# Front stage of an attention and expert kernel: query and key rows stored by three transfers each, weights on ScalarE's queue, VectorE's first work reordered

## The chip, the cores and the metric

The kernel runs on one core of one Trainium2 chip. A core has TensorE (PE in the profile), VectorE (DVE), ScalarE (ACT), GpSimd (POOL) and SyncE (SP); each has a queue of its own instructions, taken in the order in which they are written, and they meet through semaphores. SP and ACT can also issue DMAs, which move data between the chip's memory (HBM) and the core's on-chip memory (SBUF). The metric is the device time of one execution in microseconds (us); the time given for a kernel is the median of several executions that are not profiled.

## The reference

Two sequences of 1024 tokens with 128 channels go through one transformer layer. Attention has 16 heads of 8 channels, is causal, and each score gets a rank-one bias; the second half is a mixture of seven experts, of which each token takes two, with a shared expert.

```python
def _L0_attn_ref(x, w_qkv, w_out, head_scales, head_dirs):
    q, k, v = split_heads(x @ w_qkv)
    scores = jnp.einsum('bhqd,bhkd->bhqk', q, k) * SCALE
    q_proj = jnp.einsum('bhtd,hd->bht', q[..., :8], head_dirs)
    k_proj = jnp.einsum('bhtd,hd->bht', k[..., :8], head_dirs)
    scores = where(causal, scores, -inf) + head_scales * q_proj[..., :, None] * k_proj[..., None, :]
    return merge_heads(softmax(scores) @ v) @ w_out
...
x = x + _layernorm(_L0_attn_ref(_layernorm(x), ...))
x = x + _layernorm(_L0_ffn_ref(_layernorm(x), ...))   # router, top 2 of 7 experts, shared expert
```

## The kernel before, in words

There are two blocks, one after the other. The first holds the front stage and the attention, the second the projection of the second sequence, the router and the experts. The change is in the front stage.

**The front stage.** SP loads x in two transfers, one for each sequence b, and then six weights (L246, L250). VectorE's first instruction (L664, `dirs_scaled`) waits for all six. Then it computes the variances of sequence 0 (`variances(0)`, L673 to L678), folds the bias into the query weights with two small matmuls of TensorE (L391, L394; `fold`, `wq_fold`), normalises the tokens of sequence 0 (`normalise_tokens`, L691, tile `xn_stage`) and does `variances(1)` and `normalise_tokens(1)`. TensorE turns the tokens (L406), ScalarE takes them (L588, `xn_t`), and TensorE makes queries, keys and values (L415, L417, L422) for each sequence and each half of 512 tokens.

**The split in three.** Each float32 query or key is written as a sum of three bfloat16 numbers. ScalarE takes the high part (L595, L597), VectorE the middle and the low one with three instructions (L718, L721, L723), one round for the queries and one for the keys of each of four (b, half): eight rounds in all. `parts_ready` rises once for each (b, half). A product of two such numbers is kept to six of the nine pairs of parts (`COMBOS`), so each head has rows of 8 channels times 6 pairs, 48 in all, for queries and for keys, and one bfloat16 matmul over 48 rows gives a score.

**Through HBM.** The parts lie with channels on partitions; a matmul needs the 48 rows of one head on neighbouring partitions. So SP stores the parts to two arrays in HBM, `q_rows` and `k_rows` (`store_parts`, L256: six transfers for queries and six for keys of one (b, half), of 128 KB each, one for each pair), and loads them again as stacks (`load_stacks(n, c)`, L265: four transfers for a group n of four heads and a half c of the tokens). A load waits until all stores of its (b, half) have landed (`parts_stored`).

**The attention.** For each group n, TensorE first forms the scores with queries on partitions (`maxima`, L444 to L450), and VectorE takes the maximum of each row (L749). The maxima are turned, GpSimd splits them in three parts (`split_rows`, L355 to L360), and SP writes them as three more rows of the query stacks (`send_rows(n, c)`, L275: six transfers of 2 KB). Then TensorE forms the scores again with keys on partitions, less the maxima (`score`, L461), ScalarE takes exponentials (L611), and TensorE multiplies with the values (L480). Twelve units x make up a group: units 0 to 3 need the queries of half 0, units 4 to 11 those of half 1. The maxima of group 0 are formed ahead of everything else; those of group n + 1 are formed between the scores of group n. Before its first maxima TensorE waits until all splits are done (`parts_ready`, L536).

**The order of SP's queue** is written out by hand:

```python
store_parts(0, 0)
sp.wait_ge(ones_ready, STACKS)
load_stacks(0, 0)
store_parts(0, 1)
load_stacks(0, 1)
load_stacks(1, 0)
load_stacks(1, 1)
send_rows(0, 0)
for half in range(2):
    store_parts(1, half)
send_rows(0, 1)
```

Meanwhile GpSimd clears tiles (`v_pad`, `k_st`) and makes masks, until 18.8 us.

Of the kernel before, what the change touches and what calls it, by code (L numbers as in the profile page):

```python
# [16 lines left out]
BF16 = mybir.dt.bfloat16  # L17
U32 = mybir.dt.uint32
ALU = mybir.AluOpType
# [3 lines left out]
B, T, C, H = 2, 1024, 128, 16  # L23
HD = C // H
SCALE = 1.0 / float(np.sqrt(HD))
P = 128
KT = T // P
NT = B * KT
HG = 4
# [4 lines left out]
COMBOS = ((0, 0), (0, 1), (0, 2), (1, 0), (1, 1), (2, 0))  # L34
KR = HD * len(COMBOS)
MR = KR + 3
HALF = P // 2
BANK = 512
# [77 lines left out]
def program(nc, x, wqkv, wq_t, dirs, scales, w_out, router_t, w_gate, w_up, w_down, out):  # L116
    ctx = ExitStack()
    with ctx:
# [10 lines left out]
        q_rows = nc.dram_tensor("q_rows", [B * H, KR, T], BF16, kind="Internal").ap()  # L129
        k_rows = nc.dram_tensor("k_rows", [B * H, KR, T], BF16, kind="Internal").ap()  # L130
# [4 lines left out]
        w_out_sb = sb("w_out_sb", [C, C])  # L135
        router_sb = sb("router_sb", [C, E])
# [13 lines left out]
        wqkv_sb = sb_front("wqkv_sb", [C, 3 * C])  # L150
        wq_t_sb = sb_front("wq_t_sb", [C, C])
        wq_fold = sb_front("wq_fold", [C, C])
        dirs_sb = sb_front("dirs_sb", [1, C])
        scales_sb = sb_front("scales_sb", [1, H])
        dirs_scaled = sb_front("dirs_scaled", [1, C])
# [10 lines left out]
        rest = x2[:, :, :].rearrange("p t c -> p (t c)").rearrange("p (h i t) -> p h i t", h=2, i=2)  # L166
# [17 lines left out]
        def bank(i, n=1):  # L184
            return banks[:, i * BANK:(i + n) * BANK]
# [11 lines left out]
        vector_steps = sem("vector_steps")  # L197
# [46 lines left out]
        def _(sp):  # L244
# [3 lines left out]
            for dst, src in ((dirs_sb[:, :], dirs), (scales_sb[:, :], scales), (wq_t_sb[:, :], wq_t),  # L248
                             (wqkv_sb[:, :], wqkv), (w_out_sb[:, :], w_out), (router_sb[:, :], router_t)):
                sp.dma_start(dst, src).then_inc(weights_loaded, 16)  # L250

            def store_parts(b, half):
                sp.wait_ge(parts_ready, b * 2 + half + 1)
                for qk, dst in ((0, q_rows), (1, k_rows)):
                    for row, combo in enumerate(COMBOS):
                        sp.dma_start(  # L256
                            dst[b * H:(b + 1) * H, row * HD:(row + 1) * HD, half * BANK:(half + 1) * BANK],
                            parts[b][:, half, qk, combo[qk], :]).then_inc(parts_stored[b * 2 + half], 16)

            def load_stacks(n, c):  # L260
                r, b = n % STACKS, n // NG
                sp.wait_ge(parts_stored[b * 2 + c], 16 * 2 * len(COMBOS))
                for dst, src in ((q_st[r], q_rows), (k_st[r], k_rows)):
                    for a in range(2):
                        sp.dma_start(  # L265
                            dst[a * HALF:a * HALF + KR, c, :, :],
                            src[n * HG:(n + 1) * HG, :, c * BANK:(c + 1) * BANK].rearrange(
                                "(p a) r t -> a r p t", a=2)[a]).then_inc(stacks_loaded[r][c], 16)
# [119 lines left out]
        def _(pe):  # L388
# [10 lines left out]
            for b in range(B):  # L399
# [9 lines left out]
                for half in range(2):  # L409
# [3 lines left out]
                    if done >= 2:  # L413
                        pe.wait_ge(parts_ready, done - 1)
# [121 lines left out]
            pe.wait_ge(parts_ready, 4)  # L536
# [41 lines left out]
        def _(act):  # L578
            def standard_deviations(b):
                act.wait_ge(var_ready, b + 1)  # L580
                part = slice(b * KT, (b + 1) * KT)
                nc.scalar.activation(std[:, part], var_eps[:, part], ACT.Sqrt).then_inc(std_ready, 1)

            standard_deviations(0)
# [76 lines left out]
        def _(dve):  # L661
            step = Count()
            dve.wait_ge(weights_loaded, 16 * 6)
            nc.vector.tensor_tensor(dirs_scaled[:, :].rearrange("o (h d) -> o h d", d=HD),  # L664
                                    dirs_sb[:, :].rearrange("o (h d) -> o h d", d=HD),
                                    scales_sb[:, :].unsqueeze(2).broadcast_to([1, H, HD]),
                                    ALU.mult).then_inc(dirs_scaled_ready, 1)
# [28 lines left out]
            variances(0)  # L696

# [11 lines left out]
            variances(1)  # L709
            normalise_tokens(1)  # L710
            for b in range(B):
                for half in range(2):
                    for qk in range(2):
                        src = bank(4 * half + 1 + qk)
                        high, mid, low = (parts[b][:, half, qk, i, :] for i in range(3))
                        left = rest[:, half, qk, :]
                        dve.wait_ge(high_ready, b * 4 + half * 2 + qk + 1)
                        nc.vector.tensor_tensor(left, src, high, ALU.subtract  # L718
                                                ).then_inc(vector_steps, step.one())
                        dve.wait_ge(vector_steps, step.now())  # L720
                        nc.vector.tensor_copy(mid, left).then_inc(vector_steps, step.one())  # L721
                        dve.wait_ge(vector_steps, step.now())
                        last = nc.vector.tensor_tensor(low, left, mid, ALU.subtract)  # L723
                    last.then_inc(parts_ready, 1)
# [833 lines left out]
```

## Time and profile before

| | |
|---|---|
| time, median of 3 executions | 524.5 us (523.02 to 527.57) |
| span of the profiled execution | 542.4 us |
| TensorE busy | 440.5 us (81% of the span) |
| VectorE busy | 329.6 us (61%) |
| ScalarE busy | 244.3 us (45%) |
| GpSimd busy | 142.2 us (26%) |
| DMAs of SP's queue for `q_rows` and `k_rows` | 48 of 128 KB |
| first score of group 0 (L461) | 67.0 us from the span's start |

The profiled execution was 17.9 us longer than the median of the executions without a profile. Busy times are those of one execution. All stretches below are counted from the span's start; the front stage and the first group's maxima fill roughly its first 67 us, the other groups run until about 315 us, the experts until the end.

### The profile page before, as it was taken

The numbers are of one execution on the slowest core, as the hardware profiler recorded it, in microseconds if no ns is written. First come the engines' busy times: TensorE is split into PE (matmuls) and PEld (weight loads), VectorE is DVE, ScalarE is ACT, GpSimd is POOL, SyncE is SP. The second block draws the span as 40 slices with busy tenths as digits, with TensorE's granted clock in tenths as the row PEclk, the third lists the DMA queues.
The fourth block names the chain that finished last, engine by engine and source line by source line (L and its number), as shares of the span: only waits on it lengthen the run. The fifth ranks groups of instructions, "written<-read, shape, count | busy, mean of one in ns | idle before, by whom it ended". The sixth has DMA issues, their size and how long they took to land. (4 is left out here: it accounts for less than half of the span.)

```text
span 542.4 us, 10816 instructions
## 1 busy us (share of the span) xinstructions
PE 440.5 (81%) x3980; PEld 267.0 (49%) x3980; DVE 329.6 (61%) x885; ACT 244.3 (45%) x432; POOL 142.2 (26%) x211
## 2 busy tenths in 40 slices
PE   1845978989898998999898968888699989898800
PEld 0522432434434352434434345645499889888800
DVE  3975956868787876878782764599223322223356
ACT  1520145666665765677675827552122222213330
POOL 9300000010111101011111002424626665573423
PEclk9975576999989997999988988999979999999965
DMA  3065254100202020000000008100447768766352
GB/s 102 21 179 150 78 157 119 58 5 3 60 2 61 2 60 2 2 3 3 3 2 2 1 2 232 39 2 1 160 137 228 205 194 215 215 206 190 98 160 78
DMA packets 44616, 46.60 MB, mean 86 GB/s; under 512 B 6355, under 2 KB 33364, under 8 KB 44564
## 3 DMA queue, kind: packets, MB, share of 16 engines
q1 hardware_dynamic: 42132, 40.92, 25.8%
q0 software_dynamic: 2432, 4.99, 3.6%
q8 instruction: 33, 0.54, 0.4%
q14 instruction: 19, 0.16, 0.1%
HBM read 34.80 MB, written 10.88 MB: 84 GB/s over the span
## 5 line engine op out<-in xcount | busy, mean ns | idle before, releaser
L611 ACT ACTIVATE probs<-banks 128x1024 f32<-128x1024 f32 (+1 forms) x192 | 145.3, 810 | 80.6 <-PE banks L468 52.5
L749 DVE TENSOR_REDUCE mx_part<-banks 128x1 f32<-128x512 f32 (+3 forms) x256 | 133.2, 584 | 42.1 <-PE banks L444 34.2
L444 PE MATMUL banks<-k_st,q_st 48*128 48x512 bf16 (+3 forms) x384 | 123.9, 370 | 14.5 <-DMA k_st<-k_rows 12.3
L461 PE MATMUL banks<-q_st,k_st 51*128 51x512 bf16 (+3 forms) x384 | 103.7, 349 | 17.7 <-DMA q_st<-mx_rows 11.3
L480 PE MATMUL banks<-probs,v_pad 128*32 128x512 f32 (+3 forms) x768 | 86.8, 526 | 0.0
L461 PEld LDWEIGHTS banks<-q_st,k_st 51*128 51x128 bf16 x384 | 32.1, 96 | 75.7 <-ACT probs L611 49.9
L749 DVE TENSOR_REDUCE mx<-banks 128x1 f32<-128x512 f32 (+3 forms) x128 | 54.7, 485 | 20.1 <-PE banks L450 20.0
L1488 DVE TENSOR_TENSOR hidden<-banks,gate 128x512 f32<-128x512 f32 x38 | 26.3, 692 | 61.6 <-ACT gate L1256 28.8
L355 POOL TENSOR_TENSOR mx_rest<-mx_neg,mx_rows 16x128 f32<-16x128 f32 x16 | 6.7, 417 | 199.2 <-ACT mx_neg L621 199.2
L444 PEld LDWEIGHTS banks<-k_st,q_st 48*128 48x128 bf16 x384 | 34.7, 95 | 43.6 <-DVE mx_part L749 24.8
L448 PE MATMUL banks<-mask_qk,ident_half 64*128 64x128 bf16 x256 | 56.2, 232 | 0.0
L1024 POOL DMA_INDIRECT results<-result,target x38 | 37.4, 984 | 49.9 <-DVE result L1496 44.3
L466 PE MATMUL banks<-mask_kq,ident_half 64*128 64x128 bf16 x256 | 49.8, 221 | 0.0
L450 PE MATMUL banks<-mask_qk,ident_half 64*128 64x64 bf16 x256 | 49.1, 198 | 0.0
L1155 PE MATMUL banks<-rows_t,w_g 128*128 128x128 f32 x304 | 42.1, 282 | 4.4 <-issue 3.9
L468 PE MATMUL banks<-mask_kq,ident_half 64*128 64x64 bf16 x256 | 44.1, 190 | 0.0
L1164 PE MATMUL banks<-w_d,hidden 128*128 x304 | 41.0, 278 | 3.2 <-DVE hidden L1488 2.8
L1155 PE MATMUL banks<-rows_t,w_u 128*128 128x128 f32 x304 | 41.4, 279 | 0.5 <-issue 0.5
L1016 POOL DMA_INDIRECT rows<-tokens,source x38 | 36.8, 969 | 19.0 <-issue 11.0
L1155 PEld LDWEIGHTS banks<-rows_t,w_g 128*128 128x128 f32 x304 | 37.7, 195 | 6.8 <-issue 5.9
L1249 ACT ACTIVATE rows_t<-banks 128x128 f32<-128x128 f32 x38 | 10.6, 279 | 65.3 <-PE banks L1143 45.3
L1164 PEld LDWEIGHTS banks<-w_d,hidden 128*128 128x128 f32 x304 | 37.5, 194 | 4.0 <-issue 4.0
(198 smaller groups left out, 616.1 us busy)
## 6 DMA issues: line engine op xcount, KB each, us to landing
w_g<-in_w_gate SPq DMA_DIRECT2D x38, 256.0 KB
w_u<-in_w_up SPq DMA_DIRECT2D x38, 256.0 KB
q_rows<-parts SPq DMA_DIRECT2D x24, 128.0 KB, 2.4
k_rows<-parts SPq DMA_DIRECT2D x24, 128.0 KB, 2.4
q_st<-q_rows SPq DMA_DIRECT2D x32, 96.0 KB, 2.3
k_st<-k_rows SPq DMA_DIRECT2D x32, 96.0 KB, 2.3
w_d<-in_w_down SPq DMA_DIRECT2D x8, 256.0 KB, 4.9
back<-results SPq DMA_DIRECT2D x8, 256.0 KB, 4.8
```

Source lines behind the costliest of these rows:

```text
L444: last = nc.tensor.matmul(dst[:, 0:width], q_st[r][rows, c, p, (i % CH) * P:(i % CH + 1) * P], k_st[r][rows, kc, p, 0:width], start=True, ...
L448: nc.tensor.matmul(dst[:, diagonal:width], ident_half[half, 0, :], mask_qk[half, 0, :], start=False, stop=False)
L450: last = nc.tensor.matmul(dst[:, diagonal + HALF:width], ident_half[half, 1, :], mask_qk[half, 1, HALF:], start=False, stop=True)
L461: last = nc.tensor.matmul(dst[a][:, 0:width], k_st[r][rows, j // CH, p, (j % CH) * P:(j % CH + 1) * P], q_st[r][rows, c, p, first:BANK], s ...
L466: nc.tensor.matmul(dst[a][:, 0:P], ident_half[half, 1, :], mask_kq[half, 1, :], start=False, stop=False)
L468: last = nc.tensor.matmul(dst[a][:, 0:HALF], ident_half[half, 0, :], mask_kq[half, 0, 0:HALF], start=False, stop=True)
L480: last = nc.tensor.matmul(o_bank[h * HQ:(h + 1) * HQ, first:BANK], v_pad[:, n, j, h, :], probs[unit % PROBS][:, h, first:BANK], start=(x i ...
L611: nc.scalar.activation(probs[unit % PROBS][:, 2 * p:2 * p + 2, first:BANK], slot_pair[k % 2].rearrange("p (a t) -> p a t", a=2)[:, :, 0:BA ...
L749: nc.vector.tensor_reduce(dst, max_bank[m % RING][:, 0:width], AX.X, ALU.max, negate=True).then_inc(max_taken, 1)
L1024: nc.gpsimd.indirect_dma_start(results, bass.IndirectOffsetOnAxis(ap=target[:, k:k + 1], axis=0), result[i][:, :], None).then_inc(result_s ...
L1155: last = nc.tensor.matmul(dst[k % 2][:, t * P:(t + 1) * P], w[i][:, t * P:(t + 1) * P], rows_t[k % 2][:, :], start=True, stop=True)
L1164: last = nc.tensor.matmul(down_bank[k % 2][:, 0:P], hidden[k % 2][:, t, :], w_d[:, bass.ds(e, 1), t, :].rearrange("p e c -> p (e c)"), sta ...
```

## The change

- `store_parts` issues three transfers for the queries and three for the keys of one (b, half), not six and six (`RUNS`: 3, 2 and 1 pairs). The pairs of one run share the query's part, so that part is read 3, 2 or 1 times by a source that repeats; the key's parts of a run lie side by side in SBUF. The bytes that are written stay the same. The arrays in HBM are laid out by channel and pair now, and the loads of the stacks read the same number of rows of 1024 bytes.
- `parts_ready` rises after the queries and again after the keys, and the stores of the queries no longer wait for the keys' split.
- The six weights are issued by ScalarE's queue, not by SP's behind x.
- VectorE does `variances(0)` first and then waits for the weights; the split of the first (b, half) goes ahead of `normalise_tokens(1)`.

```diff
+RUNS = ((0, 3), (3, 2), (5, 1))
...
-        q_rows = nc.dram_tensor("q_rows", [B * H, KR, T], BF16, kind="Internal").ap()
-        k_rows = nc.dram_tensor("k_rows", [B * H, KR, T], BF16, kind="Internal").ap()
+        q_rows = nc.dram_tensor("q_rows", [B * C, len(COMBOS), T], BF16, kind="Internal").ap()
+        k_rows = nc.dram_tensor("k_rows", [B * C, len(COMBOS), T], BF16, kind="Internal").ap()
...
-            for dst, src in ((dirs_sb[:, :], dirs), (scales_sb[:, :], scales), (wq_t_sb[:, :], wq_t),
-                             (wqkv_sb[:, :], wqkv), (w_out_sb[:, :], w_out), (router_sb[:, :], router_t)):
-                sp.dma_start(dst, src).then_inc(weights_loaded, 16)
-
             def store_parts(b, half):
-                sp.wait_ge(parts_ready, b * 2 + half + 1)
                 for qk, dst in ((0, q_rows), (1, k_rows)):
-                    for row, combo in enumerate(COMBOS):
-                        sp.dma_start(
-                            dst[b * H:(b + 1) * H, row * HD:(row + 1) * HD, half * BANK:(half + 1) * BANK],
-                            parts[b][:, half, qk, combo[qk], :]).then_inc(parts_stored[b * 2 + half], 16)
+                    sp.wait_ge(parts_ready, b * 4 + half * 2 + qk + 1)
+                    rows = dst[b * C:(b + 1) * C, :, half * BANK:(half + 1) * BANK]
+                    for at, count in RUNS:
+                        if qk == 0:
+                            src = parts[b][:, half, 0, COMBOS[at][0], :].unsqueeze(1).broadcast_to([P, count, BANK])
+                        else:
+                            src = parts[b][:, half, 1, 0:count, :]
+                        sp.dma_start(rows[:, at:at + count, :], src).then_inc(parts_stored[b * 2 + half], 16)
...
-                sp.wait_ge(parts_stored[b * 2 + c], 16 * 2 * len(COMBOS))
+                sp.wait_ge(parts_stored[b * 2 + c], 16 * 2 * len(RUNS))
...
-                            src[n * HG:(n + 1) * HG, :, c * BANK:(c + 1) * BANK].rearrange(
-                                "(p a) r t -> a r p t", a=2)[a]).then_inc(stacks_loaded[r][c], 16)
+                            src[n * HG * HD:(n + 1) * HG * HD, :, c * BANK:(c + 1) * BANK].rearrange(
+                                "(p a d) r t -> a (d r) p t", a=2, d=HD)[a]).then_inc(stacks_loaded[r][c], 16)
...
                     if done >= 2:
-                        pe.wait_ge(parts_ready, done - 1)
+                        pe.wait_ge(parts_ready, 2 * (done - 1))
...
-            pe.wait_ge(parts_ready, 4)
+            pe.wait_ge(parts_ready, 8)
...
+            for dst, src in ((dirs_sb[:, :], dirs), (scales_sb[:, :], scales), (wq_t_sb[:, :], wq_t),
+                             (wqkv_sb[:, :], wqkv), (w_out_sb[:, :], w_out), (router_sb[:, :], router_t)):
+                act.dma_start(dst, src).then_inc(weights_loaded, 16)
             standard_deviations(0)
...
             variances(0)
+            scale_directions()
...
             normalise_tokens(0)
             variances(1)
+            split_parts(0, 0)
             normalise_tokens(1)
...
+            split_parts(0, 1)
+            split_parts(1, 0)
+            split_parts(1, 1)
```

`scale_directions` is the old first instruction of VectorE with its wait for the weights; `split_parts(b, half)` is the old pair of rounds for one (b, half), with `parts_ready` raised at the end of each round.

## Rows read from the trace of the kernel before

**Rows 1.** The page: the span; TensorE's granted clock in 40 slices.

```profile
span 542.4 us, 10816 instructions
...
PEclk9975576999989997999988988999979999999965
```

**Rows 2.** Timeline, TensorE: start, us, instruction [idle before <-what ended it].

```profile
29.91 1.05 PE L422 MATMUL banks<-wqkv_sb,xn_t 128*128 128x128 f32 x8
37.72 0.62 PE L444 MATMUL banks<-k_st,q_st 48*128 48x512 bf16 x2 [6.75 <-DMA k_st<-k_rows]
...
50.56 1.03 PE L444 MATMUL banks<-k_st,q_st 48*128 48x512 bf16 x3 [5.54 <-DMA k_st<-k_rows]
...
83.34 0.58 PE L461 MATMUL banks<-q_st,k_st 51*128 51x512 bf16 x1 [5.13 <-DMA q_st<-mx_rows]
```

**Rows 3.** Timeline, SP's queue: start, us until all are issued.

```profile
24.43 3.86 SPq L256 DMA_DIRECT2D q_rows<-parts  x6
28.33 3.86 SPq L256 DMA_DIRECT2D k_rows<-parts  x6
34.03 0.83 SPq L265 DMA_DIRECT2D q_st<-q_rows  x2
...
46.68 0.78 SPq L265 DMA_DIRECT2D q_st<-q_rows  x2
...
57.18 4.20 SPq L275 DMA_DIRECT2D q_st<-mx_rows  x6
61.42 3.80 SPq L256 DMA_DIRECT2D q_rows<-parts  x6
...
78.10 4.06 SPq L275 DMA_DIRECT2D q_st<-mx_rows  x6
```

**Rows 4.** Timeline, VectorE, 7 to 36 us.

```profile
7.82 0.28 DVE L664 TENSOR_TENSOR dirs_scaled<-dirs_sb,scales_sb 1x128 f32<-1x128 f32 x1 [7.82 <-DMA router_sb<-in_router_t]
...
10.37 1.01 DVE L678 TENSOR_SCALAR var_eps<-mean_var 128x8 f32<-128x8 f32 x1
...
13.05 2.68 DVE L691 TENSOR_SCALAR xn_stage<-x_sb,mean_var,rstd 128x128 f32<-128x128 f32 x8
...
18.68 2.14 DVE L691 TENSOR_SCALAR xn_stage<-x_sb,mean_var,rstd 128x128 f32<-128x128 f32 x8
20.74 0.68 DVE L718 TENSOR_TENSOR x<-banks,parts 128x512 f32<-128x512 f32 x1
...
34.44 0.69 DVE L723 TENSOR_TENSOR parts<-x,parts 128x512 bf16<-128x512 f32 x1
```

**Rows 5.** Tile x_sb: its loads' issue (ns) and landing.

```profile
L246 SPq DMA_DIRECT2D x_sb<-in_x x2: 450/511/572, 0.8 to 1.3; - x2
...
DMA to landing us min/median/max: 4.2/4.8/5.5
```

**Rows 6.** Timeline, GpSimd.

```profile
10.40 3.65 POOL L319 MEMSET v_pad<- 128x1024 f32 x4
...
71.94 0.42 POOL L360 TENSOR_TENSOR mx_rows<-mx_rest,mx_rows 16x128 bf16<-16x128 f32 x1
```

**Rows 7.** Timeline, ScalarE, 0 to 36 us.

```profile
18.80 0.60 ACT L595 ACTIVATE parts<-banks 128x512 bf16<-128x512 f32 x1 [0.40 <-PE banks L415]
20.24 0.60 ACT L597 ACTIVATE parts<-banks 128x512 bf16<-128x512 f32 x1 [0.84 <-PE banks L417]
```

**Rows 8.** Windows: engines' busy us (PE first), granted clock, DMA share, GB/s.

```profile
28.00:30.00 2.00, 1.88 (x5) 0.95 (x6) 1.93 (x4) 1.36 (x5) 0.00 (x0) 1.00 0.75 210
...
537.00:538.00 1.00, 0.00 (x0) 0.00 (x0) 1.00 (x4) 0.00 (x0) 0.00 (x0) 0.50 0.94 273
```

**Rows 9.** Timeline, TensorE: first scores of three units (0/7, 1/4, 1/7).

```profile
93.46 0.39 PE L461 MATMUL banks<-q_st,k_st 51*128 51x512 bf16 x1
...
115.78 0.37 PE L461 MATMUL banks<-q_st,k_st 51*128 51x512 bf16 x1 [1.65 <-DMA q_st<-mx_rows]
...
124.11 0.39 PE L461 MATMUL banks<-q_st,k_st 51*128 51x512 bf16 x1
```

More of the change, by code:

```diff
@@ L662, in _, with scale_directions @@
             step = Count()
[L663 to L667, printed above, removed]
+            def scale_directions():
+                dve.wait_ge(weights_loaded, 16 * 6)
+                nc.vector.tensor_tensor(dirs_scaled[:, :].rearrange("o (h d) -> o h d", d=HD),
+                                        dirs_sb[:, :].rearrange("o (h d) -> o h d", d=HD),
+                                        scales_sb[:, :].unsqueeze(2).broadcast_to([1, H, HD]),
+                                        ALU.mult).then_inc(dirs_scaled_ready, 1)
             def variances(b):
@@ L709, in _, with split_parts @@
             variances(1)
-            normalise_tokens(1)
[L711 to L724, printed above, removed]
+            def split_parts(b, half):
+                for qk in range(2):
+                    src = bank(4 * half + 1 + qk)
+                    high, mid, low = (parts[b][:, half, qk, i, :] for i in range(3))
+                    left = rest[:, half, qk, :]
+                    dve.wait_ge(high_ready, b * 4 + half * 2 + qk + 1)
+                    nc.vector.tensor_tensor(left, src, high, ALU.subtract
+                                            ).then_inc(vector_steps, step.one())
+                    dve.wait_ge(vector_steps, step.now())
+                    nc.vector.tensor_copy(mid, left).then_inc(vector_steps, step.one())
+                    dve.wait_ge(vector_steps, step.now())
+                    nc.vector.tensor_tensor(low, left, mid, ALU.subtract).then_inc(parts_ready, 1)
+            split_parts(0, 0)
+            normalise_tokens(1)
+            split_parts(0, 1)
+            split_parts(1, 0)
+            split_parts(1, 1)
             def merge_maxima(n):
```

## The prediction

> **What bounds the kernel now.** The chain of work that ended last reaches back only to the second block, so what the front stage costs is read from TensorE's own waits. Its timeline comes first: three times in the first 84 us it stands still for a DMA, 6.75 us before its first maxima, 5.54 us before the maxima of the second half and 5.13 us before unit 4 of group 0, 17.4 us in all [rows 2]. The first two are ended by the loads of the stacks, the third by the rows of maxima that SP sends.
>
> Then SP's queue, to see why each came late. *First wait:* the twelve stores of (0, 0) are issued from 24.43 to 32.19 us, 0.64 us each; the queue wakes from their landing at 34.03, 1.84 us after the last issue; TensorE starts 3.69 us later [rows 2, 3]. *Second:* the same with (0, 1); the loads go out at 46.68 and TensorE starts 3.88 us later. *Third:* GpSimd has the rows ready at 71.94 + 0.42 = 72.36 us [rows 6], but SP issues them at 78.10, since from 61.42 on it works through the 24 stores of sequence 1 [rows 3].
>
> Last, what paces a store. During the stores the 16 DMA engines are busy 0.75 of the time and move 210 GB/s; near the end of the kernel one store of 512 KB reaches 273 GB/s at 0.94 [rows 8]. So the engines have room, and the issue is what a store waits for. An issue's length doesn't follow its rows: the loads of x, of 1024 rows of 512 bytes (8 tiles by 128 partitions), took 0.45 and 0.57 us [rows 5], a store of 128 rows 0.64.
>
> After the front stage TensorE is the engine that the others wait for, and later SP loads wait for its progress (`slot_filled`). So I carry a shift of group 0 through to the end, one for one.
>
> **The change part by part.**
>
> *Weights on ScalarE's queue, variances first.* VectorE starts at 7.82 us, when the weights are there; the first x has landed at about 0.8 + 4.2 = 5.0 us [rows 4, 5]. The statistics of sequence 0 take from 8.10 to 10.37, 2.3 us, and now lie under the weights' load. ScalarE issues six small loads at up to 0.57 us each [rows 5], 3.4 us, ahead of a square root that it can't start before about 7.5; that hides them. Against it: the same bytes share the same engines, and if x landed as late as the weights nothing would be gained. What is late next is GpSimd. The 8-column `var_eps` took 1.01 us and ended at 11.38, just behind the first of four `v_pad` memsets of 0.91 us that begin at 10.40; the first eight `xn_stage` took 2.68 us, overlapping only the last memset, the second eight 2.14 [rows 4, 6]. Begun two microseconds earlier, the first eight meet three memsets. Of 2.3 us I keep 0.9 (bounds 0.3 and 1.9: all but the memsets' tail lost, or one wait of about 0.4 us).
>
> The Trainium skill's page "SBUF — State Buffer", section "Who interferes with whom", says that a VectorE instruction of such a kind and a GpSimd instruction exclude each other for the whole of the one that was issued first. Read strictly, with each `xn_stage` held by the next memset, only the 0.3 us would remain by my estimate, and the gain below would be 0.6 us less; the rows show the waiting, not how many pass between two memsets.
>
> *The first split ahead of `normalise_tokens(1)`.* ScalarE has the first high query part at 18.80 + 0.60 = 19.40 us and the key's at 20.84 [rows 7]; VectorE took them at 20.74, after the second `xn_stage`. Eight rounds run from 20.74 to 35.13, 1.80 us each [rows 4]. New, in the old clock: queries 19.45 to 21.25, keys to 23.05, then the reciprocal and eight `xn_stage` (2.3 us) to 25.4, then six rounds to 36.2. Less 0.9 that is 35.3, against 35.13 before. This matters, since TensorE's first maxima also wait for all splits (L536), a wait that the loads cover today, until 37.72. It is the next thing to be late: TensorE starts at about 35.4, and only 2.3 of the first 6.75 us are won.
>
> *Half as many stores.* Query stores of (0, 0) can start at 21.25 - 0.9 = 20.3 us. One (b, half) is 1.57 MB, 5.8 us at 273 GB/s [rows 8]; six issues at 0.64 take 3.9 and fit under that. Landing: 20.3 + 5.8 + 1.84 = 27.9. Four loads, twice 0.83 and gaps, go out until 29.7 and have landed by 31.6, hidden under the splits until 35.4. Stores of (0, 1): 29.7 + 5.8 + 1.84 = 37.3, loads landed 3.88 later, 41.2. TensorE's first-half maxima took from 37.72 to 50.56 - 5.54 = 45.02, 7.3 us, so they end at 42.7: the second wait goes, with 1.5 us to spare. Call X the start of the second-half maxima: 50.56 before, 42.7 now. **Gain so far 7.8 us** (2.3 and 5.5).
>
> *The third wait.* All of it is counted from X. The sends of (0, 0) go out at X + 6.6 and the stores of sequence 1 start at X + 10.9 as before [rows 3]; 3.15 MB at 273 GB/s keep the engines until X + 22.4, not the queue until X + 27.5. The rows of (0, 1) are split at X + 21.8 and land with TensorE's start 5.24 us after their first issue, at X + 27.0 to 27.6. TensorE comes to unit 4 at 83.34 - 5.13 = 78.21, X + 27.65. So hardly a wait is left; I leave 1.65 us, which the same place costs in group 1, where SP has nothing else to do [rows 9]. **Gain 3.5 us** (up to 5.1).
>
> *TensorE's clock.* Units 4 to 6 of group 0 took 10.12 us (83.34 to 93.46), those of group 1 8.33 [rows 2, 9]. The granted clock was at its lower level, 1.2 GHz, for most of the former's slice (digit 6) and at the upper for the latter's [rows 1]; it had fallen after the third wait. Without that wait it may stay up, worth 0 to 1.8 us: **0.9**.
>
> *The rest.* The two layouts in HBM give the loads the same rows of 1024 bytes at the same steps, so I price them at nothing; the repeated source costs reads in SBUF of bytes that were read as often before. `parts_ready` counts twice as fast with the same meaning.
>
> Sum: 7.8 + 3.5 + 0.9 = 12.2 us. The profiled execution would span 542.4 - 12.2 = 530.2. It lies 17.9 us above the median of 524.5, and no row tells where; I take the microseconds as they are: 524.5 - 12.2 = **512.3**.
>
> **The rivals.**
>
> *Issue time follows the rows.* 0.64 us for 128 rows and 0.42 for 96 (a load, [rows 3]) are both near 5 ns a row; then three transfers take as long as six, 7.7 us for a (b, half). For it: that ratio. Against: x's 1024 rows in half a microsecond, and the 273 GB/s store. Then X = 20.3 + 7.7 + 1.84 + 1.85 + 7.7 + 1.84 + 3.88 = 45.1, a gain of 5.4, and the third wait stays but for some 0.6 us: 524.5 - 6.0 = 518.5. It decides above 6.5 us for a (b, half), where the second wait returns.
>
> *TensorE slow on sequence 1.* It now waits some 2 us for the second `xn_stage`. If the clock fell there as it does after 29.91 + 1.05 (digit 7, then 5 [rows 1, 2]), three steps of about 1 us for each half double and the splits end at about 38.0: X = 45.4, 2.7 less, 515.0. Against: there it fell after the whole of TensorE's work had ended; here work lies on both sides of the gap.
>
> *The waits are the profile's.* The 17.4 us of waits and the 17.9 us between span and median are strangely alike. If executions without a profile didn't have these waits, nothing would be won: 524.5. Against: they follow from issues of 0.64 us, one after the other, which need no profiler.
>
> *Slower: the query transfers run on few engines.* Their source repeats a row 3, 2 or 1 times. If the count, not the 128 partitions, spread a transfer over the engines, one engine would carry a third of 384 KB, half of 256 and all of 128, 384 KB in all; at 210 / 0.75 / 16 = 17.5 GB/s [rows 8] that is 22.5 us for a (b, half) in place of 5.8. With D for that time X = 29.7 + 2D and unit 4 starts at X + 16.1 + 2D: 135.8 against 83.34, so 52 us more, 577. The two meet at D = 9.4 us, or 167 GB/s: with nine engines or fewer the change loses. Against: the source as written has its 128 partitions outermost, the repeat behind them. The Trainium skill, "DMA: Bandwidth & Descriptors", section "Why a DMA increments its semaphore by 16 and not by 1", has such a rule: the slowest dimension of both sides sets how many of the 16 engines take part. By it 128 partitions give all 16; no row here shows a transfer that repeats its source.
>
> **How the numbers follow.** Forecast 0.60, rows 0.17, slow TensorE 0.12, profile's waits 0.07, few engines 0.04. The forecast's own bounds are 10.7 us (0.3 for the start, no clock) and 15.7 (1.9, 5.1 and 1.8), so 508.8 to 513.8; the shown runs differ by up to 3 us from their median, which widens the low end to 507. To leave out no more than two in ten the range goes up to the first rival: 507 to 519. One per cent, 5.2 us, is about what a measurement of this kernel can tell from no change. Faster by more: the forecast and nearly all of the two next, 0.87. Within: 0.08. Slower: 0.05.
>
> **What would show it.** Right: stores with six issues of about 0.6 us and some 270 GB/s; the first loads issued near 28 us; TensorE's first maxima near 35.4, released by VectorE's last split, not by a load; no wait in front of the second-half maxima; the first sends of (0, 1) within a microsecond of GpSimd's last split; unit 4 after at most 1.7 us. Wrong: issues of 1 us and more (rows), splits with gaps for ScalarE's parts (clock), a DMA share far below 0.9 during the query stores (engines), or units of later groups that take longer than before and give the shift back.

## The result, and the profile of the changed kernel

The changed kernel took 508.58 us (median of 5, 507.37 to 519.39) against 523.02 us in the same session (5, 518.91 to 527.57): ratio 0.9736, 95% interval 0.9679 to 0.9794. A second series gave 506.95 against 525.78 us, 0.9666 (0.9615 to 0.9717). The forecast was 512.3 us, range 507 to 519. Some executions of either kernel are longer at a lower mean clock, the first profiled one of the changed kernel among them (519.39 us; 0.890, c1 0.924); the ratios leave them out, the medians don't (without them the second series has 523.6 us for the kernel before).

Below, c1 is the changed kernel once more, from the second series; its profiled execution took 507.31 us, and all rows of the changed kernel are those of c1. Up to the start of group 1 the two traces of the changed kernel agree within 0.9 us (90.22 and 89.33 there); in later groups they part by more. So stages are compared up to there only, and each trace is one execution: a difference of less than 0.9 us between the points of two traces proves nothing by itself.

The page of c1, its span and the granted clock in 40 slices of 12.6 us:

```profile
span 505.6 us, 10792 instructions
...
PEclk9995589979999899999999996999999999999955
```

TensorE's timeline of c1, with the points that answer to [rows 2, 9]: first maxima, maxima of the second half (X), units 4 and 7 of group 0, group 1.

```profile
35.23 0.40 PE L444 MATMUL banks<-k_st,q_st 48*128 48x512 bf16 x2 [4.22 <-DVE parts L727]
...
42.21 1.05 PE L444 MATMUL banks<-k_st,q_st 48*128 48x512 bf16 x3
...
69.94 0.39 PE L461 MATMUL banks<-q_st,k_st 51*128 51x512 bf16 x1
...
78.17 0.39 PE L461 MATMUL banks<-q_st,k_st 51*128 51x512 bf16 x1
...
89.33 0.39 PE L461 MATMUL banks<-q_st,k_st 51*128 51x512 bf16 x1
```

Of the three waits one is left, and what ends it is no longer a load but VectorE's last split (L727). The other two rows carry no bracket. Group 1 began at 104.62 us before:

```profile
104.62 0.39 PE L461 MATMUL banks<-q_st,k_st 51*128 51x512 bf16 x1
```

So 15.3 us are won by its start. They divide at the same points as in the forecast: 8.35 at X (50.56 to 42.21), 5.05 more at unit 4 (83.34 to 69.94), 1.89 more at unit 7 (93.46 to 78.17), and nothing behind it.

SP's queue of c1, against [rows 3] (start, us until all are issued):

```profile
20.41 1.57 SPq L258 DMA_DIRECT2D q_rows<-parts  x3
22.19 2.12 SPq L258 DMA_DIRECT2D k_rows<-parts  x3
27.01 0.81 SPq L265 DMA_DIRECT2D q_st<-q_rows  x2
...
28.80 1.70 SPq L258 DMA_DIRECT2D q_rows<-parts  x3
30.55 2.24 SPq L258 DMA_DIRECT2D k_rows<-parts  x3
34.89 0.80 SPq L265 DMA_DIRECT2D q_st<-q_rows  x2
...
48.80 4.23 SPq L275 DMA_DIRECT2D q_st<-mx_rows  x6
53.08 1.65 SPq L258 DMA_DIRECT2D q_rows<-parts  x3
...
59.33 2.25 SPq L258 DMA_DIRECT2D k_rows<-parts  x3
64.00 4.05 SPq L275 DMA_DIRECT2D q_st<-mx_rows  x6
```

A (batch, half) is stored and landed in 6.6 us (20.41 to 27.01) where it took 9.6 (24.43 to 34.03). And the stores of sequence 1 are issued by 59.33 + 2.25 = 61.58 us, so that the queue is idle when the rows of maxima of (0, 1) come: GpSimd has them at 63.56 + 0.42 = 63.98, SP sends them at 64.00. Before, the queue came 5.7 us late.

```profile
63.56 0.42 POOL L360 TENSOR_TENSOR mx_rows<-mx_rest,mx_rows 16x128 bf16<-16x128 f32 x1
```

Windows of c1 (busy us of each engine, granted clock, DMA share, GB/s), in the stores of (0, 0) and of sequence 1:

```profile
22.00:24.00 2.00, 1.21 (x11) 0.93 (x9) 1.96 (x9) 1.22 (x5) 0.00 (x0) 1.00 1.03 344
...
57.00:59.00 2.00, 2.00 (x20) 1.54 (x20) 1.95 (x8) 0.00 (x0) 0.00 (x0) 0.50 1.03 344
```

The DMA engines are busy all the time at 344 GB/s; [rows 8] had 0.75 and 210. An issue no longer sets the pace of a store, the engines do: 2.24 us for three transfers of 0.79 MB together are 350 GB/s.

VectorE of c1, against [rows 4]:

```profile
4.97 1.65 DVE L678 BATCH_NORM_STATS2 stats<-x_sb 128x6 f32<-128x128 f32 x8 [4.97 <-DMA x_sb<-in_x]
...
7.82 0.28 DVE L669 TENSOR_TENSOR dirs_scaled<-dirs_sb,scales_sb 1x128 f32<-1x128 f32 x1
...
10.99 3.90 DVE L696 TENSOR_SCALAR xn_stage<-x_sb,mean_var,rstd 128x128 f32<-128x128 f32 x8
...
18.50 0.69 DVE L722 TENSOR_TENSOR x<-banks,parts 128x512 f32<-128x512 f32 x1 [1.15 <-ACT parts L598]
...
34.48 0.69 DVE L727 TENSOR_TENSOR parts<-x,parts 128x512 bf16<-128x512 f32 x1
```

The statistics start 3.1 us earlier and take the place in which VectorE waited for the weights. The first `xn_stage` starts 2.06 us earlier (13.05 to 10.99) but takes 3.90 us in place of 2.68, so its end is won by only 0.84. The splits end at 35.17, as before at 35.13.

### The profile page after: what moved, and what is told of

Read it like the earlier page. It is cut to its first block and busy times, and to the rows that moved or that the text cites. A ratio compares the mean times of both kernels' runs of the same rounds, so it can differ in the third digit from the quotient of the medians.

```text
span 517.6 us, 10792 instructions
## 1 busy us (share of the span) xinstructions
PE 441.1 (85%) x3980; PEld 266.1 (51%) x3980; DVE 332.1 (64%) x885; ACT 247.1 (48%) x432; POOL 142.5 (28%) x211
## 5 line engine op out<-in xcount | busy, mean ns | idle before, releaser
L444 PE MATMUL banks<-k_st,q_st 48*128 48x512 bf16 (+3 forms) x384 | 126.6, 376 | 6.5 <-DVE parts L727 4.2
L461 PE MATMUL banks<-q_st,k_st 51*128 51x512 bf16 (+3 forms) x384 | 105.9, 354 | 12.9 <-DMA q_st<-mx_rows 6.4
L480 PE MATMUL banks<-probs,v_pad 128*32 128x512 f32 (+3 forms) x768 | 90.1, 544 | 0.0
L461 PEld LDWEIGHTS banks<-q_st,k_st 51*128 51x128 bf16 x384 | 32.4, 96 | 71.2 <-ACT probs L614 50.0
L444 PEld LDWEIGHTS banks<-k_st,q_st 48*128 48x128 bf16 x384 | 35.1, 96 | 35.9 <-DVE mx_part L758 25.1
L1025 POOL DMA_INDIRECT rows<-tokens,source x38 | 36.8, 969 | 19.0 <-issue 11.3
L1164 PE MATMUL banks<-rows_t,w_g 128*128 128x128 f32 x304 | 40.2, 275 | 0.0
L1164 PE MATMUL banks<-rows_t,w_u 128*128 128x128 f32 x304 | 40.2, 275 | 0.0
L1164 PEld LDWEIGHTS banks<-rows_t,w_u 128*128 128x128 f32 x304 | 37.0, 192 | 0.0
```

The source lines that it names most:

```text
L444: last = nc.tensor.matmul(dst[:, 0:width], q_st[r][rows, c, p, (i % CH) * P:(i % CH + 1) * P], k_st[r][rows, kc, p, 0:width], start=True, ...
L461: last = nc.tensor.matmul(dst[a][:, 0:width], k_st[r][rows, j // CH, p, (j % CH) * P:(j % CH + 1) * P], q_st[r][rows, c, p, first:BANK], s ...
L480: last = nc.tensor.matmul(o_bank[h * HQ:(h + 1) * HQ, first:BANK], v_pad[:, n, j, h, :], probs[unit % PROBS][:, h, first:BANK], start=(x i ...
L1164: last = nc.tensor.matmul(dst[k % 2][:, t * P:(t + 1) * P], w[i][:, t * P:(t + 1) * P], rows_t[k % 2][:, :], start=True, stop=True)
```

## The experiments

All times are medians; ratios are to the kernel before on the same chip. Points are the same as above, in us; X is the start of the second-half maxima, as in the prediction.

```
kernel                       first  X      unit 4  unit 7  group 1  time    ratio (95% interval)
before                       37.72  50.56  83.3    93.5    104.6    -       1
c1 changed                   35.23  42.21  69.9    78.2    89.3     506.95  0.9666 (0.9615-0.9717)
e10 before + layout          35.49  46.18  75.6    86.9    98.3     515.31  0.9844 (0.9785-0.9904)
e1  before + layout + three  34.99  43.05  71.2    79.4    90.5     511.90  0.9732 (0.9675-0.9788)
e2  changed, six transfers   35.02  41.99  71.6    82.9    94.3     514.90  0.9781 (0.9720-0.9841)
e7  changed, split behind    34.20  41.47  69.9    78.1    89.3     510.15  0.9694 (0.9637-0.9750)
e3  changed, weights on SP   34.98  41.96  69.6    77.8    89.0     510.76  0.9723 (0.9660-0.9786)
e8  before, sends first      37.72  50.22  78.6    86.9    107.2    530.20  1.0124 (1.0068-1.0180)
e4  changed, memsets late    33.59  40.56  68.4    76.6    87.8     508.87  0.9726 (0.9676-0.9776)
e5  changed, GpSimd splits   32.05  39.41  67.2    76.6    87.8     508.33  0.9716 (0.9667-0.9765)
e5b e5, first split behind   31.59  39.72  67.5    75.7    86.9     510.00  0.9758 (0.9710-0.9807)
e6  e4 and e5                30.77  38.09  65.5    73.7    84.9     504.87  0.9601 (0.9525-0.9676)
e6b e6, beside c1            30.39  37.73  65.6    75.0    86.1     504.51  0.9629 (0.9584-0.9675)
```

e1, e2, e7 and e8 shared one chip, e4 to e6 a second, e10, e3, c1 and e6b a third. Intervals overlap for everything between 0.967 and 0.976, so within that band the points of the timeline decide and not the times.

**e1: the stores alone.** The kernel before, with the new layout, the three transfers and nothing else of the change.

```
+RUNS = ((0, 3), (3, 2), (5, 1))
-q_rows [B * H, KR, T]
+q_rows [B * C, len(COMBOS), T]
-for row, combo in enumerate(COMBOS): sp.dma_start(dst[b * H:(b + 1) * H, row * HD:..., ...], ...)
+for at, count in RUNS: sp.dma_start(rows[:, at:at + count, :], src)
```

> The kernel before with only the three transfers for queries and three for keys; weights on SP's queue, VectorE's order and one ready signal for each half as before. Theory: what binds the start is VectorE's last split, which ends at 35.13 us in the old order, and the stores only have to land before it. Stores of the first half start at 24.4 us and land about 6.1 us later, at 30.5; loads have landed at 34.2, still under the splits; first maxima at 35.3, second-half maxima without a wait at 42.6, unit 4 of group 0 near 71, so all of the gain of the whole change, 13 to 14 us. Rival: the early first split and the queries stored ahead of the keys carry part of it; then the second-half maxima start 2 to 4 us later than in the changed kernel and the gain is 10 us or less.

0.9732, and group 1 at 90.5: the stores alone give 14.1 of the 15.3 us at group 1. At X, where no wait was stated, TensorE still waits 0.75 us for a load:

```profile
43.05 0.61 PE L448 MATMUL banks<-k_st,q_st 48*128 48x512 bf16 x2 [0.75 <-DMA k_st<-k_rows]
...
90.55 0.39 PE L465 MATMUL banks<-q_st,k_st 51*128 51x512 bf16 x1
```

The order of VectorE's work and the weights' queue bring 0.8 us at X by c1 and 0.5 by the first trace of the changed kernel (42.55).

**e2 and e10: six transfers again.** e2 is the changed kernel with six transfers for each operand, e10 the kernel before with the new layout and six; both write single rows of 1 KB per channel, at one step from channel to channel.

```
-RUNS = ((0, 3), (3, 2), (5, 1))
+ONE = ((0, 1), (1, 1), (2, 1), (3, 1), (4, 1), (5, 1))
-    src = parts[b][:, half, 1, 0:count, :]
+    src = parts[b][:, half, 1, COMBOS[at][1]:COMBOS[at][1] + 1, :]
```

> The changed kernel with six transfers each again (same layout in HBM, same order of VectorE, queries ahead of keys, weights on ScalarE's queue). Theory: an issue costs about 0.64 us however many rows it has, so a half takes 7.7 us of SP's queue again: first maxima at 35.3 as in the changed kernel, loads of the second half landed near 45, a wait of 2 to 3 us, second-half maxima near 45.2; the third wait of about 5 us is back, so 5 to 6 us faster than the kernel before and 8 to 9 us slower than the changed one. Rival (order carries the gain): within 3 us of the changed kernel.

The miss of the study: X came at 41.99, not 45.2, with all twelve transfers. e10 was made to see the layout by itself.

> The kernel before with the new layout in HBM alone: twelve stores for a (batch, half) as before, each of 128 rows of 1 KB, but written at one step per channel. Theory (the layout shortens an issue from 0.64 to 0.48 us, the number of transfers does the rest): stores from 24.4 us, twelve issues in 5.8 us, loads at about 32, second loads landed at about 45.2, which is where the second-half maxima start (50.56 before, 43.05 with three transfers); the 24 stores of sequence 1 end near 69, a wait of 1 to 2 us for rows of maxima is left, group 1 starts near 97 (104.6 before, 90.5 with three transfers): 7 to 8 us faster than the kernel before. Rival (the layout alone is the gain, six or three makes no difference): within 2 us of the kernel with three transfers in the old order, 12 to 14 us faster than before. Rival (only fewer transfers help, the short issue belonged to the new order of the work): issues of 0.64 us and the time of before within 1%.

SP's queue of e10, then TensorE's timeline of it:

```profile
24.42 2.78 SPq L262 DMA_DIRECT2D q_rows<-parts  x6
27.25 2.91 SPq L262 DMA_DIRECT2D k_rows<-parts  x6
31.61 0.81 SPq L269 DMA_DIRECT2D q_st<-q_rows  x2
...
42.41 0.79 SPq L269 DMA_DIRECT2D q_st<-q_rows  x2
```

```profile
46.18 0.61 PE L448 MATMUL banks<-k_st,q_st 48*128 48x512 bf16 x2 [3.39 <-DMA k_st<-k_rows]
...
75.55 0.37 PE L465 MATMUL banks<-q_st,k_st 51*128 51x512 bf16 x1 [1.47 <-DMA q_st<-mx_rows]
```

From one issue to the next, the same transfer of 128 rows from 128 partitions now takes 0.49 us (2.91 / 6), not 0.64 (3.86 / 6, [rows 3]); what differs is its pattern in HBM, which was 16 heads by 8 channels and is now 128 channels at one step. It isn't a backlog of earlier stores: the very first store of (0, 0), alone, was issued in 0.65 us before, in 0.33 in e10, and in 0.37 in c1, where it has three times the rows. These three rows, and last the third store of c1, which has 128 rows:

```profile
24.43 0.65 SPq L256 DMA_DIRECT2D q_rows<-parts  x1
24.42 0.33 SPq L262 DMA_DIRECT2D q_rows<-parts  x1
20.41 0.37 SPq L258 DMA_DIRECT2D q_rows<-parts  x1
21.35 0.62 SPq L258 DMA_DIRECT2D q_rows<-parts  x1
```

The engines gain by the layout too: in e10's stores they moved 268 GB/s while busy 0.81 of the time, before 210 while busy 0.75 [rows 8], which for engines busy all the time would be 331 and 280.

```profile
28.00:30.00 2.00, 1.95 (x6) 0.96 (x6) 1.93 (x4) 1.38 (x5) 0.00 (x0) 1.00 0.81 268
```

The layout alone gives 0.9844 and 6.3 us at group 1; three transfers in place of six give another 7.8 (98.3 to 90.5). Both figures include what the clock did in units 4 to 6, which took 10.1 us before, 11.3 in e10 and 8.2 in e1. Up to unit 4 the layout gives 7.8 us and the three transfers 4.4 (83.3, 75.5, 71.2). With the changed order of the work the six cost 5.0 us at group 1 (94.3 against 89.3), of which 1.6 stand at unit 4. The theory named for e10 holds, with X 1.0 us later than stated. In e2 the rows of maxima show why the number still matters: SP is in the stores of sequence 1 until 65.88 and sends late, and TensorE waits 1.69 us again; its clock then stood at 1.2 GHz from 73.7 to 83.9 us, and units 4 to 6 took 11.3 us, in c1 8.2.

```profile
61.72 4.16 SPq L258 DMA_DIRECT2D k_rows<-parts  x6
65.92 4.47 SPq L275 DMA_DIRECT2D q_st<-mx_rows  x6
```

```profile
71.55 0.37 PE L461 MATMUL banks<-q_st,k_st 51*128 51x512 bf16 x1 [1.69 <-DMA q_st<-mx_rows]
```

Three transfers in the old layout weren't tried: there the rows of a channel lie apart from each other by all channels of a head, so heads, channels and rows are three steps in HBM, in the new layout two. Whether the merging alone would have done as much stays open.

**e7: the first split behind the second normalisation**, where it stood before; otherwise the changed kernel.

```
-split_parts(0, 0)
 normalise_tokens(1)
+split_parts(0, 0)
 split_parts(0, 1)
```

> The changed kernel with the first split behind the second normalisation again. Theory: the early split only moves 2.3 us of normalisation into the row of splits that ends last; without it the eight splits run without a gap and end near 34.7, the first stores go out about 1.5 us later and are still hidden: first maxima 34.8, second-half maxima 42.1, so 0 to 0.7 us faster than the changed kernel. Rival: the early stores are needed, second-half maxima wait for their loads and the kernel is 1 to 2 us slower than the changed one.

X is earlier by 0.5 to 1.1 us than in the four traces that have the new order and all splits on VectorE (41.96 to 42.55: e3, e2, c1 and the first one of the changed kernel). So the new order seems to cost about that much at X: it sends the stores earlier, but the loads are hidden now, and the splits that bind end 1.0 us later in c1 (35.17, here 34.14). At group 1 both stand at 89.3, and the times don't separate them.

**e3: the weights back on SP's queue**, behind the loads of x.

```
-act.dma_start(dst, src).then_inc(weights_loaded, 16)
+sp.dma_start(dst, src).then_inc(weights_loaded, 16)
```

> The changed kernel with the six weights back on SP's queue, behind the two loads of x. Theory (the start is gained because VectorE's statistics no longer wait for the weights, not because of the queue that carries them): the statistics start near 5.0 us as in the changed kernel, the scaled directions within 0.5 us of 8.04, the second-half maxima within 0.3 us of 42.55, the time within 1% of the changed kernel. Rival (the second queue brings the weights sooner): the last weight lands 1 us later or more, and the fold, the first normalisation and the second-half maxima are later by as much.

VectorE starts its statistics at 4.92 us and the scaled directions at 7.77, c1 at 4.97 and 7.82; X is 41.96, 0.6 us earlier than stated. The time is within 1% of c1, as stated. The queue that carries the weights is worth nothing that these rows show; what is gained at the start comes from VectorE no longer standing in front of them.

**e8: what the third wait is made of.** The kernel before, with the sends of (0, 1) ahead of the stores of sequence 1; nothing else.

```
+send_rows(0, 1)
 for half in range(2): store_parts(1, half)
-send_rows(0, 1)
```

> The kernel before with one move in SP's queue: the sends of the maxima of (0, 1) ahead of the stores of sequence 1. Theory: first and second wait as before (first maxima 37.7, second-half maxima 50.6), third wait from 5.1 us to 0 to 1.7, and the clock doesn't fall in units 4 to 6: unit 7 of group 0 near 87 in place of 93.5, so 5 to 7 us faster than the kernel before. Rival (the third wait isn't SP's queue but the engines being busy with the stores): the wait stays above 3 us. Second rival: the wait goes, but the clock falls all the same, then 3.5 to 5 us.

The wait goes, as the forecast's step had it (unit 7 at 86.9, 6.6 us earlier), and the kernel is slower all the same (1.0124), where 5 to 7 us less had been stated. SP's queue of e8, and TensorE's row at group 1:

```profile
56.84 19.24 SPq L275 DMA_DIRECT2D q_st<-mx_rows  x12
76.13 3.79 SPq L256 DMA_DIRECT2D q_rows<-parts  x6
...
101.92 4.07 SPq L275 DMA_DIRECT2D q_st<-mx_rows  x6
```

```profile
107.16 0.58 PE L461 MATMUL banks<-q_st,k_st 51*128 51x512 bf16 x1 [9.06 <-DMA q_st<-mx_rows]
```

The queue now waits for GpSimd's rows, the stores start at 76.13 instead of 61.42, and the loads and sends of group 1 stand behind them until 101.92. The wait of 5.13 us has become one of 9.06. Here reordering the full queue moved the wait; shorter stores took it away.

**e4, e5, e5b: what holds the first maxima now.** The profile of the changed kernel names VectorE's splits. e4 clears the second sequence's value tiles behind the masks, so that GpSimd is out of the way of the first `xn_stage`; e5 gives GpSimd the middle and low parts of sequence 1, and VectorE its subtractions only; e5b is e5 with e7's order.

```
e4  -for b in range(B): (memsets of v_pad)
    +clear_values(0); (masks); clear_values(1)
e5  +if b == 1: nc.vector.tensor_tensor(left, src, high, subtract).then_inc(left_ready, 1); continue
    +nc.gpsimd.tensor_copy(mid, left); nc.gpsimd.tensor_tensor(low, left, mid, subtract)
    -pe.wait_ge(parts_ready, 8)
    +pe.wait_ge(parts_ready, 4); pe.wait_ge(left_ready, 4)
```

> The changed kernel with GpSimd's four memsets of the second sequence's values behind its masks, so that they begin near 13.6 us, not at 10.4. Theory: in the changed kernel the first eight normalisations took 3.78 us since each pair waited for a memset; without memsets beside them they take about 2.2, the splits end 1.5 us earlier (33.7), first maxima near 33.8, second-half maxima near 41.0, so 1 to 1.5 us faster than the changed kernel. Rival (the normalisations were slow for another cause, and the later memsets only hit something else, such as the second variances): 0 to 0.3 us, or slower.

> The changed kernel with the middle and low parts of sequence 1 made by GpSimd (idle from 19 to 48 us), so that VectorE does one instruction of three in the last four rounds; TensorE's first maxima wait for VectorE's four instructions, which free the banks. Theory: what binds the first maxima is VectorE's row of splits; 4 times 1.1 us go from it, but the high parts of the last half come only near 30 us, so first maxima near 31.6, second-half maxima when their loads land, near 38.9 (42.6 in the changed kernel): 3 to 3.7 us faster than the changed kernel. Rival (something else than VectorE binds, the clock or the loads): second-half maxima later than 41.5 and less than 1 us.

> The same with the first split behind the second normalisation, as before the change. Theory: once VectorE's row of splits no longer ends last, the loads do, and then the early first split pays: loads of the second half land 0.6 us later here than with the early split, second-half maxima near 39.5, so 0.5 to 1 us slower than the run with the early split, though with all splits on VectorE the late place was the faster one by 1.1 us. Rival (the order doesn't matter once the splits are short): equal within 0.3 us in the start of the second-half maxima.

All three move X to within about 0.5 us of what was stated: 40.56, 39.41, 39.72. In e4 the first eight `xn_stage` take 2.14 us, not 3.90, from the same start; the memsets had cost 1.76 us. In e5b the stores come later, and TensorE's first rows of the second half wait 1.11 us for a load again, as stated. But X is only 0.3 us later than in e5, less than two traces of one kernel differ by, so that with short splits the early first split costs nothing, and that it pays isn't shown. At group 1 the three are 1.6, 1.5 and 2.5 us ahead of c1 (in e5 the clock fell in units 4 to 6, which took 9.4 us); their times, where more had been stated for e5, can't be told from the changed kernel's.

**e6 and e6b: both together.**

> The changed kernel with both: memsets behind the masks and sequence 1's middle and low parts on GpSimd. Theory: the two add, since the earlier normalisation moves stores and loads too: second-half maxima near 37.6, 4.5 to 5 us faster than the changed kernel, about 504. Rival (GpSimd's memsets, masks and splits get into each other's way or into VectorE's): no better than the run with the splits on GpSimd alone.

> The changed kernel as it is, for a comparison on one chip: 508 to 511 us, 0.97 to 0.98 of the kernel before; the first score units at 59.0, unit 4 of group 0 at 70.8 and group 1 at 90.2 us if this execution runs the front stage as the first one did.

> The changed kernel with both additions (GpSimd clears the second sequence's value tiles behind the masks, and takes the middle and low parts of that sequence), beside the changed kernel on one chip. Theory (the second-half maxima start 4.5 us earlier, and what is gained in group 0 is kept to the end): 4 to 5.5 us below the changed kernel. Rival (the earlier difference was one between chips, as the clocks differ): within 2 us of it.

504.87 us, and beside c1 on one chip 504.51 against 506.95: 0.9629 (0.9584 to 0.9675) against 0.9666 (0.9615 to 0.9717). c1 came 1 us below what was stated for it, and the medians are 2.4 us apart, between the 4 to 5.5 of the theory and the 2 of the rival. The intervals overlap: probably the best kernel of the study, not certainly. X is 4.5 us earlier than in c1, group 1 only 3.2. Rows of e6b, VectorE, then TensorE:

```profile
10.95 2.14 DVE L711 TENSOR_SCALAR xn_stage<-x_sb,mean_var,rstd 128x128 f32<-128x128 f32 x8
```

```profile
30.39 0.40 PE L458 MATMUL banks<-k_st,q_st 48*128 48x512 bf16 x2 [1.03 <-DVE x L738]
...
37.73 0.61 PE L458 MATMUL banks<-k_st,q_st 48*128 48x512 bf16 x2 [0.33 <-DVE mx L776]
```

Up to unit 4 it is 4.4 us ahead, at unit 7 only 3.2: units 4 to 6 took 9.4 us there, 8.2 in c1, and the granted clock stood at 1.2 GHz from 69.6 to 73.0 us. So 1.2 us went to the clock; it isn't shown why it fell there in this execution. In e6 itself those units took 8.2 us.

## Why the prediction was right, step by step

**Half as many stores: right in its sum, wrong in its cause.** Stores begin at 20.41 (20.3 forecast), the first loads go out at 27.01 (27.9), the second at 34.89 (37.3), X is 42.21 (42.7): 8.35 us won where 7.8 stood. But the step held 0.64 us for the price of any transfer and priced the two layouts "at nothing". That failed: the loads' pattern stayed, as it says, but the stores' did not. e10 shows the layout by itself at 0.49 us per issue and 0.9844 of the time, 7.8 of 12.2 us up to unit 4; the number of transfers gives the rest. The sum came out all the same because it went by the engines' rate, under which six issues fit at either price. The sentence "an issue's length doesn't follow its rows" stands, but the row that it was read from, the loads of x, has another pattern than the stores. The rate was taken too low as well: 273 GB/s from a store near the end of the kernel, 344 measured.

**Weights on ScalarE's queue, variances first: right, 0.84 us at the end of the first `xn_stage` for 0.9.** GpSimd's memsets take back the rest, as the step said, and e4 shows it by taking them away. The Trainium skill, "SBUF — State Buffer", section "Who interferes with whom", has the exclusion of such instructions. The strict reading (one held by each memset, 0.3 us left) doesn't hold: single instructions of the trace end within 0.15 us of a memset's end, one at the first and two at each of the next three, and the eighth behind them. So half as many memsets as instructions were waited for, and 0.84 us remained. That the weights go by ScalarE's queue had no part in it (e3).

**The first split ahead of `normalise_tokens(1)`: right that the splits bind next.** TensorE's first maxima at 35.23 (35.4), released by L727; 2.5 of the first 6.75 us won (2.3). The order itself costs some 0.5 to 1.1 us at X (e7); the 1.1 us that VectorE's splits end later by are in the step's own numbers (36.2 against 35.13), only not set against what the early stores bring when loads are hidden, which is nothing.

**The third wait: the mechanism right, the size too small.** Rows ready at X + 21.8, as forecast; sent at once; TensorE at unit 4 at X + 27.7, without a wait. 5.05 us are won where 3.5 were taken (5.1 was the bound). The step's own sum had the rows land at X + 27.0 to 27.6, just before TensorE came at X + 27.65; the 1.65 us of wait that it left all the same were taken over from group 1, and they did not come. In group 1 of c1 the same place still waits 1.65 us (100.49). The stores were faster than the step had them, with the engines done at about 63.2 us, X + 21.0, not X + 22.4; by its own sum that is worth 0.6 us at most. e8 shows that the stores of sequence 1 are the cause, and that to move them aside is no cure.

**TensorE's clock: 1.89 us, not 0.9, and by luck.** The bound of 1.8 is what came. The kernel before fell to 1.2 GHz at about 81.3 us, inside its third wait; c1, with no wait there, stayed at 2.4 GHz through units 4 to 6. That the wait decides isn't shown. In e2 and e10 a wait of 1.69 and 1.47 us stood there and the clock fell, but in group 1 of before one of 1.65 us stood there [rows 9] and it stayed, and in e5 and e6b it fell without one. Windows of group 1 of before, then of e6b (the granted clock is the third number from the end):

```profile
115.00:124.00 9.00, 8.07 (x53) 2.44 (x53) 7.36 (x12) 6.62 (x9) 1.11 (x3) 1.00 0.00 0
70.00:72.00 2.00, 2.00 (x11) 0.31 (x5) 0.87 (x2) 0.77 (x3) 0.00 (x0) 0.50 0.73 214
```

Sum: 8.35 + 5.05 + 1.89 = 15.3 us at group 1, against 12.2; the medians moved by 14.4 and 18.8 us (16.6 without the longer executions). The carrying through "one for one" can't be tested closer than that, since the later groups differ between executions by their clock.

**The rivals.** *Issue time follows the rows* falls as it was put: the store of 384 rows is issued in 0.37 us, that of 128 rows behind it in 0.62. *TensorE slow on sequence 1* falls: the granted clock was at 2.4 GHz until 35.9 us, through the gap and the projections behind it. *The waits are the profile's* falls: the medians moved by 14.4 us, and the waits that went are 17.42 - 4.22 = 13.2. And the profiled execution of e8, whose queue is that of before up to X, took 530.56 us, hardly more than its median of 530.20, and has the first two waits too (6.75 and 5.21 us). *The query transfers run on few engines* falls with the DMA share of 1.03. The packets tell the same: the DMA view of 20 to 27 us of c1 counts

```profile
DMA packets 1633, 1.58 MB, mean 226 GB/s; under 512 B 96, under 2 KB 1632, under 8 KB 1632
```

1536 rows of 1 KB and 96 small packets for 6 transfers, 16 for each: all 16 engines (one packet more is of another queue). In the kernel before the same view has 192 for its 12, so that the old layout was not held back by fewer engines either. The Trainium skill, "DMA: Bandwidth & Descriptors", section "Why a DMA increments its semaphore by 16 and not by 1", lets each engine that takes part write one such mark; the counts agree with it.

## What to carry to other kernels

When a queue of stores is on the path, read the issue time of each shape of transfer apart, and cost both sides of the pattern: the same bytes from the same partitions were issued in 0.49 or in 0.64 us by their steps in HBM alone. Once the engines run at their full share, the issues no longer set the pace; then look at what the next release is. Before reordering a queue, count what it must carry up to the next deadline: if it has no slack, the wait only moves behind the reordered piece, and may grow.

## What the runs showed of the hardware that was not expected

- From one issue on SP to the next it took 0.64 us for 128 rows of 1 KB written as 16 by 8 in HBM and 0.49 us written as 128 at one step. Alone on the queue, an issue took 0.65 and 0.33 us for these two, and 0.37 us for 384 rows at 3 per channel. Three issues of 384, 256 and 128 rows took 0.52 us each in the mean, 0.75 once the engines were full. Why the first pattern takes longer wasn't tried further.
- Rows of 1 KB went from SBUF to HBM at 344 GB/s with all engines busy.
- VectorE's `xn_stage` passed mostly in pairs at the end of each GpSimd memset, and eight took 3.90 us in place of 2.14.
- GpSimd's middle and low part of one operand (a cast of 0.61 and a subtraction of 1.16 us) took 1.8 us, as long as VectorE's three steps, of which VectorE then kept the first (0.69).
